# Causal attention on one Trainium2 core: the mask of the scores moves from TensorE to VectorE, the copies from VectorE to ScalarE, and the ring of banks gets a regular order

## What is computed

```python
scores = jnp.einsum('bhqd,bhkd->bhqk', q, k) / HEAD_DIM ** 0.5      # 32 heads of 16, 8 key heads
causal = jnp.tril(jnp.ones((s, s), dtype=bool))
scores = jnp.where(causal[None, None], scores, -jnp.inf)
probs = jax.nn.softmax(scores, axis=-1)
out = jnp.einsum('bhqk,bhkd->bhqd', probs, v)
```

## Time and profile before

| | |
|---|---|
| median of three runs | 2932.77 us |
| the profiled execution, its own time | 2930.81 us |
| its span (first to last instruction) | 2929.1 us |
| PE busy | 2793.4 us, 95% |
| DVE busy | 1236.7 us, 42% |
| ACT busy | 877.9 us, 30% |
| attention: first to last row maximum | 189.43 to some 600 us of the span |
| mean granted TensorE clock | 0.982 of 2.4 GHz |

### The profile page before, as it was taken

The page is one execution under the profiler, slowest core; times in us unless marked ns, Lnnn a source line. Parts: engine busy times, 40 slices in busy tenths (PEclk is TensorE's granted clock), DMA queues, the critical chain, the costliest instruction groups (busy, mean ns, idle before and its releaser), DMA issues.

```text
span 2929.1 us, 45881 instructions
## 1 busy us (share of the span) xinstructions
PE 2793.4 (95%) x16150; PEld 2283.9 (78%) x16150; DVE 1236.7 (42%) x2152; ACT 877.9 (30%) x1697; POOL 838.8 (29%) x1306
## 2 busy tenths in 40 slices
PE   6989999988999939999999999999999999999998
PEld 6865555556666529999999999999999999999997
DVE  6756777747888833332232232132133133133111
ACT  1126666641555512221121121122122122122110
POOL 4546776631166641101101111011021021011010
PEclk9999999999999969999999999999999999999999
DMA  3101222242122223221122032032033033022010
GB/s 109 43 1 31 48 45 48 55 92 87 68 84 75 77 83 106 91 86 64 51 92 75 26 108 83 15 109 87 12 108 101 11 100 104 14 90 85 26 47 21
DMA packets 97078, 194.68 MB, mean 66 GB/s; under 512 B 22126, under 2 KB 23758, under 8 KB 96800
## 3 DMA queue, kind: packets, MB, share of 16 engines
q1 hardware_dynamic: 75072, 131.77, 15.1%
q0 software_dynamic: 21856, 60.73, 6.6%
HBM read 148.77 MB, written 38.94 MB: 64 GB/s over the span
## 4 chain that ended last, share of the span: by engine, by line
PE 62%; DMA 0%; POOL 0%; DVE 0%; issue 0%; ACT 0%; DVEq 0%; POOLq 0%
PE ex_hid L1775 31%; PE ex_acc L102 10%; PE ex_acc L103 10%; PE ex_acc L104 10%; PE ex_xb L1745 1%; DMA ex_ys<-xn_dram,ex_slot_gather 0%; POOL out_dram L1627 0%; POOL ex_ys L1607 0%; DVE ex_ys L1688 0%; POOL ex_xg L1592 0%; DMA ex_ys<-slot_table_dram 0%; PE ex_acc L1745 0%; DVE ex_h0l L1696 0%; ACT ex_h0h L1655 0%; DVE ex_xT0l L1671 0%
## 5 line engine op out<-in xcount | busy, mean ns | idle before, releaser
L1696 DVE SCALAR_TENSOR_TENSOR ex_h0l<-ex_hid,ex_h0h 128x640 fp32r<-128x640 f32 x128 | 105.5, 824 | 682.8 <-ACT ex_h0h L1655 682.8
L1696 DVE SCALAR_TENSOR_TENSOR ex_h1l<-ex_hid,ex_h1h 128x640 fp32r<-128x640 f32 x128 | 105.4, 824 | 602.9 <-ACT ex_h1h L1655 602.3
L1655 ACT ACTIVATE ex_h0h<-ex_hid 128x640 fp32r<-128x640 f32 x128 | 90.1, 704 | 734.5 <-PE ex_hid L1775 734.5
L1655 ACT ACTIVATE ex_h1h<-ex_hid 128x640 fp32r<-128x640 f32 x128 | 90.1, 704 | 729.8 <-PE ex_hid L1775 729.8
L654 DVE TENSOR_REDUCE at_nb<-at_ring 128x2 f32<-128x512 f32 (+1 forms) x384 | 246.8, 685 | 121.1 <-PE at_ring L760 120.9
L1597 POOL COPY ex_gi<-ex_slot_gather 128x1 int32 (+1 forms) x82 | 15.3, 187 | 918.2 <-PE ex_xb L1745 913.3
L102 PE MATMUL ex_acc<-ex_w_h,ex_h1h 128*128 128x512 f32 x640 | 254.8, 398 | 0.0
L102 PE MATMUL ex_acc<-ex_w_h,ex_h0h 128*128 128x512 f32 x640 | 253.4, 396 | 0.0
L103 PE MATMUL ex_acc<-ex_w_l,ex_h0h 128*128 128x512 f32 x640 | 250.3, 391 | 0.0
L103 PE MATMUL ex_acc<-ex_w_l,ex_h1h 128*128 128x512 f32 x640 | 250.2, 391 | 0.0
L104 PE MATMUL ex_acc<-ex_w_h,ex_h1l 128*128 128x512 f32 x640 | 249.8, 390 | 0.0
(11 more groups left out here) (273 smaller groups left out, 5665.2 us busy)
## 6 DMA issues: line engine op xcount, KB each, us to landing
ex_raw<-in_w_tiles_dram SPq DMA_DIRECT2D x256, 256.0 KB, 2.8
x_in<-in_x_dram SPq DMA_DIRECT2D x32, 256.0 KB, 2.7
act<-at_raw SPq DMA_DIRECT2D x128, 64.0 KB
at_recb<-o_rec_dram SPq DMA_DIRECT2D x16, 512.0 KB
k<-in_x_dram SPq DMA_DIRECT2D x32, 256.0 KB, 2.7
cx_ctx<-in_ctx_dram SPq DMA_DIRECT2D x16, 512.0 KB, 3.8
out_dram<-cx_res SPq DMA_DIRECT2D x16, 512.0 KB, 2.8
xn_dram<-cx_prob SPq DMA_DIRECT2D x16, 512.0 KB, 2.8
```

The lines of the kernel that those rows point to most:

```text
L1655: act.activation(h[f % 2][0][:], hid[:, :, 0:HB], ACT.Relu).then_inc(sm["h_hi"], 1)
L1696: dve.scalar_tensor_tensor(h[f % 2][1][:], hid[:, :, 0:HB], 0.0, f32(h[f % 2][0][:]), ALU.max, ALU.subtract).then_inc(sm["h_lo"], 1)
```

## The change

The mask matmuls of TensorE go. The table `mask` becomes 128 x 256: 128 columns of 0, then the triangle. VectorE now adds it and takes the maximum in one pass per head: `tensor_tensor_reduce` computes (scores + mask) x -1, writes this back in place into the PSUM bank, and keeps the minimum in one column of `at_nb`. It takes one head at a time: four passes over 128 columns for a bank of rounds 0 and 1, two over 256 columns for the others. The bank's semaphore is raised by the last of them. Each wait for scores becomes an instruction of its own. Both copies of VectorE go to ScalarE. The ring is given out as two scores, one turned bank, two scores, and so on; each round has one bank to turn.

```diff
-        TURNS = ("s0", "s1", "m", "qa", "s2", "s3", "s4", "s5", "qb", "qc", "s6", "s7", "s8", "s9", "qd", "k", "s10", "s11")
+        TURNS = ("s0", "s1", "k", "s2", "s3", "m", "s4", "s5", "qa", "s6", "s7", "qb", "s8", "s9", "qc", "s10", "s11", "qd")
...
 # ScalarE
-                    if p == 0 and within(h - 1, 0, HALVES):
+                    if p == 0 and within(h + 1, 0, HALVES):
+                        keep_k(h + 1, (2 * q + e + 1) % 4, bank(e, "k"))
+                    if p == 1 and within(h - 1, 0, HALVES):
...
-                    if p % 2 == 0 and within(h + 1, 0, HALVES):
-                        name = ("qa", "qb", "qd")[p // 2]
-                        keep_q(h + 1, (2 * q + e + 1) % 4, name, bank(e, name), p // 2)
+                    if p >= 2 and within(h + 1, 0, HALVES):
+                        name = sorted(QUERIES)[p - 2]
+                        keep_q(h + 1, (2 * q + e + 1) % 4, name, bank(e, name))
...
 # VectorE
-                            dve.wait_ge(sm["scores"], ONE + PIECES * h + n + 1)
-                            dve.tensor_reduce(nb[e][:, r, p % 2, heads, qb],
-                                              bank(e, f"s{n}")[:].rearrange("p (h k) -> p h k", h=heads.stop - heads.start),
-                                              AX.X, ALU.max, negate=True).then_inc(sm["maxima"], 1)
-                    if p == 2 and within(h + 1, 0, HALVES):
-                        keep_q(h + 1, (2 * q + e + 1) % 4, bank(e, "qc"))
-                    if p == 4 and within(h + 1, 0, HALVES):
-                        keep_k(h + 1, (2 * q + e + 1) % 4, bank(e, "k"))
+                            x = bank(e, f"s{n}")
+                            wait_apart(dve, sm["scores"], PIECES * h + n + 1, passed_dve)
+                            width, qb, heads = (P, 0, range(REP)) if p < 2 else (S, 1, range(p // 2 * 2 - 2, p // 2 * 2))
+                            for c, a in enumerate(heads):
+                                y = x[:, c * width:c * width + width]
+                                m = dve.tensor_tensor_reduce(y, y,
+                                                             t["mask"][:, S - width:S], -1.0, LARGEST, ALU.add, ALU.min,
+                                                             nb[e][:, r, p % 2, a, qb:qb + 1])
+                            m.then_inc(sm["maxima"], 1)
...
 # TensorE, score
-                        pe.matmul(banks[r][:, c, :], qs[i][rows, p % 2, n, width - P:width],
-                                  ks[i][rows, p % 2, 0:width], start=True, stop=False, skip_group_check=True)
-                for r in range(2):
-                    pe.matmul(banks[r][:, :, width - P:width], t["identb"][:],
-                              t["mask"][:].unsqueeze(1).to_broadcast([P, len(heads), P]), start=False, stop=True,
-                              skip_group_check=True).then_inc(sm["scores"], 1)
+                        m = pe.matmul(banks[r][:, c, :], qs[i][rows, p % 2, n, width - P:width],
+                                      ks[i][rows, p % 2, 0:width], start=True, stop=True, skip_group_check=True)
+                        if c == len(heads) - 1:
+                            m.then_inc(sm["scores"], 1)
...
 # TensorE, the round
-                    if p == 0 and within(h - 1, 0, HALVES):
-                        turn_m(h, e)
-                    if within(h + 1, 0, HALVES):
-                        for name in {0: ("qa",), 2: ("qb", "qc"), 4: ("qd",)}.get(p, ()):
-                            turn_q(h, e, name)
-                    if p == 4 and within(h + 1, 0, HALVES):
-                        turn_k(h, j, e)
+                    if p == 0 and within(h + 1, 0, HALVES):
+                        turn_k(h, j, e)
+                    if p == 1 and within(h - 1, 0, HALVES):
+                        turn_m(h, e)
+                    if p >= 2 and within(h + 1, 0, HALVES):
+                        turn_q(h, e, sorted(QUERIES)[p - 2])
```

More of the change, by code:

```diff
@@ L38 @@
 MASKED = -1e30
+LARGEST = 3e38
 ONE = 1
@@ L159, in _ @@
             pool.wait_ge(mask_set, ONE + 2)
-            pool.affine_select(out=t["mask"][:], in_=t["mask"][:], compare_op=ALU.is_ge, fill=MASKED, base=0,
+            pool.affine_select(out=t["mask"][:, P:S], in_=t["mask"][:, P:S], compare_op=ALU.is_ge, fill=MASKED, base=0,
                                pattern=[[-1, P]], channel_multiplier=1)
@@ L392, in stage_attention @@
         o_den, o_rec = io["o_den"], io["o_rec"]
-        names = ("q_hi", "q_stacked", "q_turned", "q_act", "q_dve", "k_turned", "k_kept", "m_turned", "m_kept", "k_hi",
+        names = ("q_hi", "q_stacked", "q_turned", "q_act", "k_turned", "k_kept", "m_turned", "m_kept", "k_hi",
                  "k_stacked", "scores", "maxima", "shifted", "probs", "masked", "v_ready", "sums",
@@ L565, in _, with keep_q @@
         def _(act):
-            def keep_q(h, i, name, x, n):
+            def keep_q(h, i, name, x):
                 act.wait_ge(sm["q_turned"], ONE + 4 * h + 1 + sorted(QUERIES).index(name))
@@ L570, in keep_q, with keep_k @@
                                scale=HD ** -0.5).then_inc(sm["q_act"], 1)
+            def keep_k(h, i, x):
+                act.wait_ge(sm["k_turned"], ONE + h + 1)
+                act.activation(ks[i][:].rearrange("p g n -> p (g n)"), x[:], ACT.Copy).then_inc(sm["k_kept"], 1)
             def keep_sums(h, qb, i, b):
@@ L578, in first @@
             def first():
-                for n, name in enumerate(("qa", "qb", "qd")):
-                    keep_q(0, 0, name, bank(1, name), n)
+                for name in ("qa", "qb", "qc", "qd"):
+                    keep_q(0, 0, name, bank(1, name))
+                keep_k(0, 0, bank(1, "k"))
             def step(j, w, q, e):
@@ L642, in first @@
                     dve.memset(x[:], 1.0).then_inc(sm["filled"], 1)
-                keep_q(0, 0, bank(1, "qc"))
-                keep_k(0, 0, bank(1, "k"))
             def step(j, w, q, e):
@@ L713, in taken @@
                     pe.wait_ge(sm["k_kept"], ONE + h + 2)
-                if last == "qc" and within(h + 1, 0, HALVES):
-                    pe.wait_ge(sm["q_dve"], ONE + h + 2)
-                if last in ("qa", "qb", "qd") and within(h + 1, 0, HALVES):
-                    pe.wait_ge(sm["q_act"], ONE + 3 * h + 4 + ("qa", "qb", "qd").index(last))
+                if last in QUERIES and within(h + 1, 0, HALVES):
+                    pe.wait_ge(sm["q_act"], ONE + 4 * h + 5 + sorted(QUERIES).index(last))
                 return bank(e, name)
@@ L791, in first @@
                     turn_q(-1, 1, name)
-                pe.wait_ge(sm["q_act"], ONE + 3)
-                pe.wait_ge(sm["q_dve"], ONE + 1)
+                pe.wait_ge(sm["q_act"], ONE + 4)
                 turn_k(-1, -1, 1)
@@ L800, in step @@
                 if live_s:
-                    pe.wait_ge(sm["q_act"], ONE + 3 * h + 3)
-                    pe.wait_ge(sm["q_dve"], ONE + h + 1)
+                    pe.wait_ge(sm["q_act"], ONE + 4 * h + 4)
                     pe.wait_ge(sm["k_kept"], ONE + h + 1)
@@ L1795, in decoder_layer @@
         t["identb"] = s.sb("identb", [P, P], BF16)
-        t["mask"] = s.sb("mask", [P, P], BF16)
+        t["mask"] = s.sb("mask", [P, S], BF16)
         t["ones"] = s.sb("ones", [P, P])
```

9 lines of the change are left out of this document (removed).

## The result

| | before | after |
|---|---|---|
| median | 2932.48 us (4 runs, 2928.07 to 2932.86) | 2977.81 us (4 runs, 2974.20 to 2981.55) |
| the profiled execution | 2930.81 us | 2978.85 us |
| mean granted TensorE clock | 0.982 | 0.959 |
| first row maximum (start) | 189.43 us | 189.90 us |
| first turned maxima copied (`at_mT`) | 201.89 us | 206.16 us |

The change makes the kernel slower: ratio 1.0159, 95% interval 1.0146 to 1.0172, which is 45 us where 20 were forecast. All of it arises in the attention stage, whose last turned maxima come 48.9 us later; from there to the end it is 2328.0 us before and 2327.1 after.

The account below looks back on a forecast made before the run. The prediction took TensorE as nearly the bound before, and VectorE's passes with hand-over waits after. It added 16 us for later halves, 3 for the first and 1 for the opening to 2930.81 us: 2951 us, range 2905 to 3035.

Parts of the forecast that it names:

- x: Attention, VectorE: cost per pass of reading the accumulated minimum, plus the new pass's extra over a plain one; taken as 0.11 us.
- the 16 us for halves 3 to 30: Attention stage after the pipeline fills: 29 halves, each 0.56 us longer, were to add 16 us.
- the 3 for halves 0 to 2: Attention's first halves, where the pipeline fills: 37.9 us for 34.8, 3 us more.
- the 1 for the opening: Start of the attention stage: five copies in a row on ScalarE were to cost about 1 us.
- the prediction's own formula: Attention, time of a half: 11.77 + 16x us for x below 0.11, 10.90 + 24x above.
- it decides from x = 0.062 down: Attention: the rival that TensorE's relief wins; x 0.05 or less gives 12.6 us a half, 2919 us; chance 0.20.
- What the hand-overs cost: Attention, rounds 3 and 5: VectorE idles 0.66 us behind each, 1.32 us a half, waiting for scores.
- The chain: Attention, rounds 3 and 5: 2.43 us from the end of a second bank's read through transpose and `values` to VectorE's start.
- The forecast of 13.54 us: Attention, a half after the change: 12.22 us of VectorE's work plus 1.32 us idle, 0.56 more than 12.98.
- TensorE's clock falls: Attention: the rival that lighter load drops TensorE to 1.2 GHz through the stage, some 200 us more; chance 0.04.
- a granted clock below 1.00 in the loop: Attention loop: a listed sign that the prediction is wrong; it expected TensorE's clock at 1.00.
- the most that TensorE can give: Attention: dropping the mask matmuls saves 1.84 us a half, 59 us over 32 halves, were TensorE alone the bound.

Follow-up runs that it names:

- experiment 7: The changed kernel with VectorE's attention loop written out and four useless TensorE matmuls in each half; 2941.94 us, ratio 1.0034.
- experiment 6: The changed kernel with four useless TensorE matmuls of 512 columns added in round 1 of each half; 2947.84 us, ratio 1.0054.
- Experiment 5: The changed kernel with the attention loop written out on VectorE alone, so without a branch there; 2962.66 us, ratio 1.0118.
- experiment 4: The changed kernel with masks on VectorE only in rounds 2 to 5; rounds 0 and 1 keep TensorE's mask matmuls and plain maxima; 2931.84 us, ratio 1.0006.
- experiment 2: The kernel before with only the new ring order and the copies on ScalarE; masks and maxima stay as before; 2918.37 us, ratio 0.9956.
- experiment 10: Ring order and copies of the change, masks and maxima as before, plus 18 useless matmuls ahead of the attention stage; 2920.25 us, ratio 0.9961.
- experiment 9: The changed kernel with VectorE's loop written out and four useless matmuls a half, plus 18 before the first bank and four per round of halves 0 and 1; 2961.77 us.
- experiment 8: The kernel before with only VectorE's two copies moved to ScalarE, old ring order, masks on TensorE; 2932.05 us, ratio 1.0000.
- experiment 3: The changed kernel with no mask on the scores for the maxima: mask matmuls and new passes left out, plain maxima; 2893.12 us, ratio 0.9874.
- experiments 11: The kernel of experiment 7 with 66 useless one-column matmuls ahead of the attention; 2959.52 us, ratio 1.0101.
- experiment 12: The kernel of experiment 9 with 62 further useless one-column matmuls ahead of the attention; 2942.66 us, ratio 1.0043.

## Why the prediction was wrong

The side was right. That 2977.81 us lies in the range (2905 to 3035) is luck: what it holds above 2972 us stood for passes with an x over 0.14, and x is 0.05. The size was not right: 45 us for 20. The sum went wrong in both directions, and the errors partly cancelled. Measured between first maxima, the 16 us for halves 3 to 30 were 40, the 3 for halves 0 to 2 were 8, and the 1 for the opening 0.5.

- **"I take x = 0.11 us".** x is 0.05. The two rows of 0.10 that it was taken from were the wrong neighbours: a small instruction of VectorE by itself and ScalarE's read. VectorE's read of its accumulator starts together with the next pass. By the prediction's own formula this is 11.77 + 16 x 0.05 = 12.57 us a half and a kernel of some 2919 us. So "it decides from x = 0.062 down" was wrong too: x lies below, and the kernel is not faster. (The "some 70 ns" of overhead per instruction does not follow from the prediction's slope: 0.605 us less 512 x 1.07 ns is 57 ns. The two steps measured after give 1.04 ns a column, and by that it is 72.)
- **"What the hand-overs cost".** The chain is the right picture: at x = 0.05 its formula has VectorE idle three times a half, and three times is what experiment 7 shows. It is short in size. It gives 12.57 us for the full clock; halves at the full clock take 12.85 to 13.3, and 13.16 on average in experiment 7. By the formula VectorE idles 2.43 - 4 x 0.38 = 0.9 us behind rounds 3 and 5 each; in the rows of experiment 7 it is 0.95 and 1.18, and the 0.12 us between two pairs comes on top. The forecast of 13.54 us lay nearer to 13.16 than its parts deserved: x was too large by 32 x 0.06 = 1.9 us of VectorE's time, and the waits too small.
- **"TensorE's clock falls ... Chance 0.04".** This is the step that failed. The prediction named the mechanism, the lighter load included, left it out of its sum and gave it next to no chance because "The new gaps are under a microsecond each". The row that it had of a low clock was of a long idle stretch, and it took that as what is needed. The runs show otherwise: the clock of 300 to 500 us is 0.87, it falls where the rows have gaps of 0.3 to 0.6 us beside rounds 0 and 1, and four useless matmuls there bring it to 0.99 and take 30 us off (experiment 6), 21 with VectorE's loop written out (experiment 7 against 5). Its price was wrong as well: it set 1.2 GHz through the whole stage (200 us), while the clock falls for some 3 or 10 us at a time and comes back. Of the prediction's own signs of being wrong, "a granted clock below 1.00 in the loop" came.
- **VectorE's loop was not looked at.** The trace has 122 records of VectorE in one pass of its loop (four halves) before and 362 after, and the prediction counted them as time alone. The branch at the loop's end stops VectorE for 2.1 to 2.3 us after, never before, and never in experiment 4, with 234 records. Experiment 5 removes the stops and 15 us; on top of the fillers it is 6 us, since the stop costs most when it takes the clock down with it. The pages of the profile have a hint of the cause: the queue named q14 instruction moves 64 packets after and 34 before, and 52 with the loop written out.
- **The first three halves.** "3 more" and an opening of 1 us; measured 8 more in experiment 7 and after. The opening itself cost nothing (the first maxima are 0.5 us later). Five of the 8 are there with the ring's order alone: experiment 2 has 39.4 us, at a clock of 0.79 in 180 to 250 us, and only 33.9 in experiment 10, at 0.94. With the new passes the clock is no more than a part: at 0.93 in experiment 9 they still take 39.0 us for 34.8.
- **Right:** the copies cost nothing (experiment 8); the other stages keep their length. That GpSimd's, the DMAs' and the waits' edits cost nothing was not tried by itself; no row points at them. The mask matmuls were rightly called the most that TensorE can give, 59 us, but less than half of it is to be had (25 us, experiment 3 against 2).
- **Missed:** that the ring's order is a gain of its own, 13 us (experiment 2). The prediction costed the ring only through the chain that goes with the new passes.

The account, from rows of this case: −13 us for the ring's order; +24 for passes and hand-overs (experiment 7 less experiment 2: 0.60 us a half, 17 in all, 3.5 in the first three halves, where the clock is low in both, the rest not placed); +36 for the clock and the stops (after less experiment 7). Sum +47, measured +45. The 24 include what the fillers themselves cost: the shortest halves at a clock of 1.00 take 12.85 us in experiment 5 and 13.02 in experiment 7. By an estimate from these, up to 28 x 0.17 = 5 us of the 24 are the fillers', and the clock and the stops cost as much more.

What isn't settled: whether VectorE's stop comes from the length of its loop or from where it lies, as TensorE's does (experiments 11 and 12 moved TensorE's code alone); and what in rounds 0 and 1 makes the clock fall, the gaps, how close they lie, or the lighter load as a whole, since the fillers close gaps and add load together.

## What to carry to other kernels

Relief of TensorE is not free by itself; here its granted clock fell from 1.00 to 0.87 with it. Where work leaves TensorE and hand-overs take its place, read the granted clock in stretches of a few microseconds, and see whether useless matmuls in the gaps make it faster. Try the parts of a change apart: here the ring's order alone (2918 us) is better than the kernel before and than the whole change, and dropping the mask ahead of the maxima (2893 us) is better still where the scores' spread allows a shift above the true maximum. And before an experiment is read in one stage, compare the others: a few dozen instructions more can move a later loop to a place where each new pass costs 3 us.

## What the runs showed of the hardware

- **The clock.** TensorE's granted clock went from 1.00 to 0.50 behind idle times of 0.33 and 0.54 us a microsecond apart (360 to 362 us), and behind one of 1.6 to 1.9 us (389 us). It stayed at 0.50 from 390 to 398 us though TensorE was busy in all of it by its record. The Trainium skill (TensorE: Matmul & The Clock Gate, "A second HAM failure mode: psum-queue depth-cycling") describes a kernel in which short idle times between groups of matmuls, as the engine turns through its PSUM banks, make the clock oscillate; this trace agrees. Neither a gap nor idle time by itself tells: in experiment 3 TensorE waits once a half, up to 0.8 us, and is busy for 186.24 of 200 us, and the clock is 1.00; in the kernel after it is busy for 16.14 of the 20 us from 780 us on, in another stage, at 1.00. No run here separates the gaps of rounds 0 and 1 from the lighter load.
- **A taken branch.** It cost VectorE 2.06 to 2.27 us in a loop of 362 trace records and showed no stop in loops of 122 and 234, and it cost TensorE 2.3 to 3.3 us or 0.2 to 0.4 us for the same loop, by its place. A shift of 66 matmuls brought the stops and one of 128 took them away. The Trainium skill (Runtime: NRT & Kernel Launch, "Instruction fetch mechanics") says that instructions are fetched in blocks of 256 and that a taken branch out of the blocks at hand stalls until its target has come; by an estimate from that, the 128 matmuls of experiment 12 with their 128 weight loads are one block, and its time, back at 2942.66 us, agrees. It gives no time for the stall; the runs do.
- **VectorE's accumulator.** The pass with an accumulated minimum and its read have a step of 0.38 us for 256 columns and 0.25 us for 128, though their durations add up to 0.60 and 0.47 us. Writing the result back to PSUM in place added nothing that can be told from this.
